# Attention weights split into bf16 pairs on the vector engine, and quantized weights stored in tiles

## The reference

```python
h = einsum('bse,end->bsnd', layernorm(x), proj_weight)      # 16 heads x 64
q = einsum('bsnd,ndh->bsnh', h, attn_weight)
scores = einsum('bsnh,brnh->bsnr', q, h) / 64
w = softmax(scores, axis=-1)
v = einsum('brnd,ndh->brnh', h, value_weight)
x = x + einsum('bsnr,brnh->bsnh', w, v).reshape(b, s, -1) @ out_w.T + out_b

def bitlinear(x, w):       # act_quant: round to 8 bits per row; weight_quant: -1, 0, 1 by mean |w|
    return einsum('bsi,oi->bso', act_quant(x), weight_quant(w))
y = layernorm(x)
x = x + bitlinear(silu(bitlinear(y, w_gate)) * bitlinear(y, w_up), w_down)
```

## Time and profile before

| | us |
|---|---|
| two timed runs | 8569.36 and 8852.18, median 8710.77 |
| the profiled execution | 8584.53 |
| its span on the slowest core (core 3) | 8583.0 |
| spans of all cores | 8447.2 to 8583.0 |
| PE busy | 5073.9 (59%) |
| DVE busy | 2923.0 (34%) |
| ACT busy | 1595.1 (19%) |
| POOL busy | 87.8 (1%) |

### The profile page before, as it was taken

One profiled execution on the slowest core, in us unless ns is written; L12 is line 12 of the kernel. 1 busy time (PEld: TensorE's weight loads), 2 busy tenths in 40 slices (PEclk: granted clock), 3 DMA queues, 4 the chain that ended last, 5 costly groups with the idle time before them and its releaser, 6 DMA issues.

```text
span 8583.0 us, 74830 instructions; the slowest of 8 cores (8447.2 to 8583.0 us)
## 1 busy us (share of the span) xinstructions
PE 5073.9 (59%) x21542; PEld 1955.8 (23%) x21542; DVE 2923.0 (34%) x6992; ACT 1595.1 (19%) x2602; POOL 87.8 (1%) x134
## 2 busy tenths in 40 slices
PE   0015568788887884447878788886354363353443
PEld 0002222222222221222222222222232232232232
DVE  5664431211112114552121212113434524434434
ACT  0000013333332331003333233331000000000000
POOL 0000000000000000000000000000000000000000
PEclk9996677878878886668889889887666566566666
DMA  7640000000000001000000000002343343343343
GB/s 265 235 153 30 30 9 2 5 1 2 4 2 2 1 2 38 30 25 4 2 4 2 5 2 2 1 2 48 71 93 71 62 102 67 66 96 68 82 86 71
DMA packets 837224, 395.55 MB, mean 46 GB/s; under 512 B 803939, under 2 KB 804067, under 8 KB 830692
## 3 DMA queue, kind: packets, MB, share of 16 engines
q1 hardware_dynamic: 827044, 353.00, 17.3%
q0 software_dynamic: 9792, 37.78, 1.2%
HBM read 352.95 MB, written 33.55 MB: 45 GB/s over the span
## 4 chain that ended last, share of the span: by engine, by line
PE 54%; DVE 24%; DMA 8%; issue 7%; DVEq 6%; ACT 0%; SPq 0%; ACTq 0%; POOLq 0%; POOL 0%
PE pb_av L766 23%; PE pb_s L785 10%; PE pb_av L466 5%; PE pf_u L1293 2%; PE pf_g L1287 2%; PE pb_av L662 2%; PE pf_d L1475 2%; PE pf_d L1293 2%; DMA f_wd<-wdq 2%; PE pf_d L1287 2%; DVE ln_lo L484 2%; DVE ln_hi L482 2%; DVE f_guq L1448 1%; DVE f_gr L1439 1%; DVE rr_t L844 1%
## 5 line engine op out<-in xcount | busy, mean ns | idle before, releaser
L826 ACT ACTIVATE w<-pb_s,cbias 128x512 f32<-128x512 f32 x2048 | 1298.0, 685 | 1673.7 <-PE pb_s L785 1673.2
L766 PE MATMUL pb_av<-w,vA 128*65 128x512 f32 x2048 | 1161.5, 650 | 0.0
L766 PE MATMUL pb_av<-w,vB 128*65 128x512 f32 x2048 | 1101.2, 621 | 0.0
L844 DVE RECIPROCAL rr_t<-pb_av 1x512 f32<-1x512 f32 x64 | 210.1, 3320 | 2306.3 <-PE pb_av L766 2306.3
L1475 PE MATMUL pf_d<-f_guq,f_wd 128*128 128x256 bf16 x2048 | 279.4, 307 | 648.2 <-DVE f_guq L1448 542.9
L785 PE MATMUL pb_s<-q_hi,h_hi 64*128 64x512 bf16 x2048 | 448.5, 409 | 260.0 <-DVEq L713 150.5
L1263 ACT ACTIVATE f_si<-f_gr 128x256 f32<-128x256 f32 x256 | 106.9, 417 | 2094.9 <-DVEq L1319 1202.5
L785 PE MATMUL pb_s<-q_lo,h_hi 64*128 64x512 bf16 x2048 | 443.3, 404 | 0.0
L766 PEld LDWEIGHTS pb_av<-w,vB 128*65 128x65 f32 x2048 | 294.9, 144 | 645.7 <-issue 645.7
L785 PE MATMUL pb_s<-q_hi,h_lo 64*128 64x512 bf16 x2048 | 441.6, 402 | 0.0
L644 DVE TENSOR_TENSOR x_tm<-x_tm,pb_av 128x512 f32<-128x512 f32 x256 | 176.1, 688 | 702.1 <-PE pb_av L662 595.7
(11 more groups left out here) (216 smaller groups left out, 5488.3 us busy)
## 6 DMA issues: line engine op xcount, KB each, us to landing
f_wg<-wgq SPq DMA_DIRECT2D x256, 256.0 KB, 3.3
f_wu<-wuq SPq DMA_DIRECT2D x256, 256.0 KB, 3.9
f_wd<-wdq SPq DMA_DIRECT2D x64, 1024.0 KB, 8.1
wraw<-wgT SPq DMA_DIRECT2D x16, 2048.0 KB, 10.4
wraw<-wuT SPq DMA_DIRECT2D x16, 2048.0 KB, 10.0
wraw<-wdT SPq DMA_DIRECT2D x64, 512.0 KB, 4.0
xa<-x_full SPq DMA_DIRECT2D x64, 512.0 KB, 3.2
x_tm<-x_full SPq DMA_DIRECT2D x16, 512.0 KB, 13.8
```

The lines of the kernel that those rows point to most:

```text
L766: last = te.matmul(pb_av[2 + hidx][0:65, 0:512], vb[:, o:o + 65], w32[:, wofs:wofs + 512], start=(rc == 0), stop=(rc == NRC - 1))
L826: a_e.inc(sc.activation(w32[:, slot:slot + 512], pb_s[hidx][:, 0:512], AFT.Exp, bias=cbias[:, 2 * scpar + hidx:2 * scpar + hidx + 1], scal ...
L844: v.reciprocal(rr_t[64:65, hidx * 512:(hidx + 1) * 512], pb_av[2 + hidx][64:65, 0:512])
```

## The change

The change has three parts.

1. The exponentials are split. For every tile of `w32` DVE makes `w_hi` (bf16) and `w_lo` (the rest, bf16), and AV becomes three bf16 matmuls per head instead of one fp32 matmul. The values become pairs too: `vA_hi`, `vA_lo`, `vB_hi`, `vB_lo`, with 1.0 and 0.0 in the last column. AV now waits for the split (`v_w`), and an exponential waits for the split that read its slot, not for AV.
2. The put-off output projection is issued at block 1 of the next loop instead of block 8. In DVE's stream the residual adds stand ahead of the new block of splits.
3. The quantized weights are stored in DRAM as `[128, blocks, row tiles, 128]`, so that the load of a block is one contiguous piece per partition, 2 KB for `f_wg` and `f_wu` and 8 KB for `f_wd`. The write of a tile by POOL now has pieces of 128 columns, 256 bytes each.

```diff
-    wgq_h = nc.dram_tensor("wgq", [E, INNER], BF16, kind="Internal").ap()
-    wuq_h = nc.dram_tensor("wuq", [E, INNER], BF16, kind="Internal").ap()
-    wdq_h = nc.dram_tensor("wdq", [INNER, E], BF16, kind="Internal").ap()
+    wgq_h = nc.dram_tensor("wgq", [128, 32, 8, 128], BF16, kind="Internal").ap()
+    wuq_h = nc.dram_tensor("wuq", [128, 32, 8, 128], BF16, kind="Internal").ap()
+    wdq_h = nc.dram_tensor("wdq", [128, 8, 32, 128], BF16, kind="Internal").ap()
...
                     o_wq.inc(g.dma_start(
-                        out=dst[t * 128:(t + 1) * 128, :],
-                        in_=wqt[:, (t % 2) * 4096:(t % 2) * 4096 + wdt]), t)
+                        out=dst[:, :, t, :],
+                        in_=wqt[:, (t % 2) * 4096:(t % 2) * 4096 + wdt]
+                        .rearrange("p (o c) -> p o c", c=128)), t)
...
-                    for (hp, vb) in ((0, vA), (64, vB)):
+                    for (hp, vh, vl) in ((0, vA_hi, vA_lo), (64, vB_hi, vB_lo)):
                         pav = pb_av[(0 if hp == 0 else 2) + rc % 2]
-                        v.tensor_copy(vb[:, o:o + 64], pav[:, 0:64])
-                        v.memset(vb[:, o + 64:o + 65], 1.0)
+                        v.tensor_copy(vh[:, o:o + 64], pav[:, 0:64])
+                        v.memset(vh[:, o + 64:o + 65], 1.0)
+                        v.drain()
+                        v.tensor_tensor(vl[:, o:o + 64], pav[:, 0:64],
+                                        vh[:, o:o + 64], ALU.subtract)
+                        v.memset(vl[:, o + 64:o + 65], 0.0)
                     v_ve.inc(v.drain())
...
                         for hidx in range(2):
-                            a_e.w(te, bae + 2 * rc + hidx + 1)
+                            v_w.w(te, bvw + 2 * rc + hidx + 1)
...
-                            last = te.matmul(
-                                pb_av[2 + hidx][0:65, 0:512],
-                                vb[:, o:o + 65],
-                                w32[:, wofs:wofs + 512],
-                                start=(rc == 0), stop=(rc == NRC - 1))
+                            for k, (vv, ww) in enumerate(
+                                    ((vh, w_hi), (vh, w_lo), (vl, w_hi))):
+                                last = te.matmul(
+                                    pb_av[2 + hidx][0:65, 0:512],
+                                    vv[:, o:o + 65],
+                                    ww[:, wofs:wofs + 512],
+                                    start=(rc == 0 and k == 0),
+                                    stop=(rc == NRC - 1 and k == 2))
...
-                        if rc == 8 and pend is not None:
+                        if rc == 1 and pend is not None:
                             emit_outproj(te, pend)
...
                             if rc >= 2:
-                                t_av.w(sc, btav + rc - 1)
-                            elif btav > 0:
-                                t_av.w(sc, btav + rc - 1)
+                                v_w.w(sc, bvw + 2 * rc - 2)
+                            elif bvw > 0:
+                                v_w.w(sc, bvw + 2 * rc - 2)
...
+                @blk.vector
+                def _(v):
+                    for rc in range(NRC):
+                        for hidx in range(2):
+                            a_e.w(v, bae + 2 * rc + hidx + 1)
+                            slot = (2 * (rc % 2) + hidx) * 512
+                            v.tensor_copy(w_hi[:, slot:slot + 512],
+                                          w32[:, slot:slot + 512])
+                            v.drain()
+                            v.tensor_tensor(w_lo[:, slot:slot + 512],
+                                            w32[:, slot:slot + 512],
+                                            w_hi[:, slot:slot + 512], ALU.subtract)
+                            v_w.inc(v.drain())
...
                         out=f_wg[:, buf:buf + 1024].rearrange("p (a c) -> p a c", c=128),
-                        in_=wgq_h[:, oc * 128:(oc + 1) * 128].rearrange(
-                            "(a p) c -> p a c", p=128)), oc)
+                        in_=wgq_h[:, oc, :, :]), oc)
...
                             "p (a c) -> p a c", c=128),
-                        in_=wdq_h[:, ec * 128:(ec + 1) * 128].rearrange(
-                            "(a p) c -> p a c", p=128)), ec)
+                        in_=wdq_h[:, ec, :, :]), ec)
```

More of the change, by code:

```diff
@@ L310, in build_program @@
         h_lo = asb("h_lo", [128, 4 * 4096], BF16)
-        vA = asb("vA", [128, NRC * 65], F32)
-        vB = asb("vB", [128, NRC * 65], F32)
+        vA_hi = asb("vA_hi", [128, NRC * 65], BF16)
+        vA_lo = asb("vA_lo", [128, NRC * 65], BF16)
+        vB_hi = asb("vB_hi", [128, NRC * 65], BF16)
+        vB_lo = asb("vB_lo", [128, NRC * 65], BF16)
         stat = asb("stat", [128, 16], F32)
@@ L560, in emit_attention @@
             (aw_f, vw_f, ow_f, aw_hi, aw_lo, vw_hi, vw_lo, ow_hi, ow_lo,
-             q_hi, q_lo, w32, mq_t, cbias, csc, crow,
+             q_hi, q_lo, w32, w_hi, w_lo, mq_t, cbias, csc, crow,
              attn_tm, attn_hi, attn_lo, rr_t, rhib, fbA_t, fbB_t, attnB_s) = T
@@ L751, in emit_attention @@
                 hm = curhead
-                bts, bae, btav = t_s.n, a_e.n, t_av.n
+                bts, bae, btav, bvw = t_s.n, a_e.n, t_av.n, v_w.n
                 bvnm, btat, bvaf = v_nm.n, t_at.n, v_af.n
@@ L763, in emit_av @@
                             wofs = (2 * (rc % 2) + hidx) * 512
-                            vb = [vA, vB][hidx]
+                            vh, vl = [(vA_hi, vA_lo), (vB_hi, vB_lo)][hidx]
                             o = rc * 65
-                            last = te.matmul(
-                                pb_av[2 + hidx][0:65, 0:512],
-                                vb[:, o:o + 65],
-                                w32[:, wofs:wofs + 512],
-                                start=(rc == 0), stop=(rc == NRC - 1))
+                            for k, (vv, ww) in enumerate(
[6 more added lines that the diff above has]
+                                    stop=(rc == NRC - 1 and k == 2))
                         t_av.inc(last)
@@ L935, in build_program @@
                      bsb("w32", [128, 4 * 512], F32),
+                     bsb("w_hi", [128, 4 * 512], BF16),
+                     bsb("w_lo", [128, 4 * 512], BF16),
                      bsb("mq_t", [128, 1], F32), bsb("cbias", [128, 4], F32),
@@ L1238, in _ @@
                         out=f_wg[:, buf:buf + 1024].rearrange("p (a c) -> p a c", c=128),
-                        in_=wgq_h[:, oc * 128:(oc + 1) * 128].rearrange(
-                            "(a p) c -> p a c", p=128)), oc)
+                        in_=wgq_h[:, oc, :, :]), oc)
                     d_fw.inc(sy.dma_start(
                         out=f_wu[:, buf:buf + 1024].rearrange("p (a c) -> p a c", c=128),
-                        in_=wuq_h[:, oc * 128:(oc + 1) * 128].rearrange(
-                            "(a p) c -> p a c", p=128)), oc)
+                        in_=wuq_h[:, oc, :, :]), oc)
             @blk.scalar
```

## The result

The change makes the kernel slower: 1.0345 times the time before, 95% interval 1.0298 to 1.0393 (medians 8577.0 us before, 8823.1 us after). The ratio leaves out executions in which some cores ran slower at a lower TensorE clock, so it isn't the quotient of the medians, which is 1.029. The profiled execution took 8871.6 us, on its slowest core (core 0) a span of 8870.1 us, against 8583.0 on core 3 before. I read the start times of each stage's first and last instruction in the trace, for these two cores and for core 5 of both. The slowest cores alone would mislead: in the first attention stage of before, cores 2 and 3 had a mean granted clock of 0.82 and the other six 0.88, and over the whole span of after, cores 0 to 3 had 0.75 and cores 4 to 7 had 0.77.

A forecast was written before the change was run, and what follows sets the result against it. The prediction took attention, and in it TensorE, to bound the kernel before. From 8585 us, loops +105, value build +160, reading -125 and writing +155 gave 8880 us, range 8700 to 9070.

The forecast's parts named there:

- Writing, +155: Weight quantization: writing tiled weights in 256 B pieces from GpSimd adds 155 us, between ends of +30 and +280.
- the middle between "all fixed" and "4.2 ns a row": GpSimd's issue of weight writes: fixed cost gives +30 us, cost per row up to +280; +155 taken.
- Rival A: Weight writes: 4096 pieces cost GpSimd as much as 128, so writing is +30, total 8755 us; chance 0.24.
- "many us" nor "still at 0.5 us": Signs in POOL's write records: many us at L287 would show the forecast right, still 0.5 us wrong.
- Records stretched by DVE: Weight writes: DVE's two-port instructions stop GpSimd's issue, as 1039 against 539 ns; 60 us more if always.
- Loops, +105: Attention loops: splits on DVE, the moved projection and slow stretches add 105 us to 3047, +65 to +145 by gap length.
- The base of the loops: Attention loops before the change: 95.2 us a loop, 3047 us in all 32, from the profiled execution.
- "DVE becomes the bound": Attention loops at full clock: splits take DVE 2.72 us a block against 2.62 before, 0.10 us slower.
- The second ring: Attention loops: split, AV, scores and exponential in line over two blocks, 2.67 us a block, just under DVE's 2.72.
- Value build, +160: Value build: more small DVE instructions make a block 1.2 us instead of 0.57, +160 us over 256 blocks.
- Reading, -125: Feed-forward weight loads in larger pieces: down projection -110 us, f_wg and f_wu -15, together -125.
- Rivals C and D: Attention loops: C, splits without gaps on DVE, -490 us, chance 0.05; D, TensorE loses full clock, about 10300 us, chance 0.04.

The follow-up runs named there:

- act_write: Kernel after with the quantized weights' writes issued from ACT's queue instead of GpSimd's; weight quantization ends at mean 597.4 us, in after 569.6.
- lag2: Kernel after with AV issued one block later and three slots a head for w_hi and w_lo; median block 2.76 us, as in after.
- spread: Kernel after with one group and one residual add of the put-off projection in each of blocks 1 to 8; ratio to before 1.0277.
- inc_sub: Kernel after without the second drain of each tile's split, the subtract itself signalling; ratio to before 1.0038.
- share: Kernel after with head A's w_hi made by ACT as a second exponential instead of DVE's cast; ratio to before 1.0337.
- vgroup: Kernel after with eight key blocks of values in one PSUM bank and DVE's four instructions once for eight blocks; 8651.6 us.

## Why the prediction was right, and where it wasn't

The direction came out: slower, by 295 us forecast and 287 between the two profiled executions (8880 and 8871.6 us). That the size did too is luck: the writing was priced 146 us too high, and the loops, the reads and two stages together as much too low.

- **Writing, +155: wrong.** It was +9 us at the stage's end (562.9 to 571.8; +7 in the mean over the cores). The step that failed is the middle between "all fixed" and "4.2 ns a row". The rows of before hinted at the first (528 ns for 64 rows, 539 for 128), and 4096 pieces take 1.64 us: (1644 - 539)/3968 = 0.28 ns a piece. Rival A had the mechanism, and of the signs neither "many us" nor "still at 0.5 us" came. Also a piece of 256 B was taken for a transfer of 256 B, and `act_write` shows that this holds for ACT's queue only. The Trainium skill, "DMA: Bandwidth & Descriptors", section "Anatomy of one DMA", says that many descriptors can be emitted before the cost shows. The trace agrees in part: 32 times as many pieces cost three times the record, 1.1 us more. The Trainium skill, "DMA: Bandwidth & Descriptors", section "SWDGE vs HWDGE vs iDMA", gives up to 4096 B as the preferred packet for DMAs issued by GpSimd. The trace agrees: the packets have 4096 B.
- **Records stretched by DVE: right, but harmless.** The median for `wgq` is 3.24 us where 1.64 is the shortest. Before it was 1.28 and 0.53. DVE's waits for the writes stayed (42.0 and 41.2 us).
- **Loops, +105: mechanism right, too small.** It is +177 against core 3. The gap behind the subtract is 187 ns (336.0 us over the 1793 casts that didn't wait for ACT), not the 166 of the earlier trace rows, and cast to subtract 76 ns: 2048 x 23 ns = 47 us. The mean block, 2.80 us, is above its median of 2.76, which makes up for the rest. The start of a loop was right to a tenth (12.1 us, forecast 2.8 + 8.6 + 0.8).
- **The base of the loops.** I took 3047 us as the kernel's own pace. It was that of cores 2 and 3 alone (3051); the other six had 2943 to 2946 us in the same execution. After has 3216 to 3231 us on all eight, though cores 0 to 3 had a granted clock of 0.82 in the first attention stage and cores 4 to 7 had 0.86: with DVE as the bound the loops hardly feel TensorE's clock. So against six of eight cores the loops lose 275 us; the earlier trace rows, where the granted clock was 0.81, described two cores of one execution. The +20 for slow stretches rests on them too.
- **"DVE becomes the bound": right.** `lag2` leaves the block as it is (the loops change by 31 us of 3228), `spread` pays for each add, `inc_sub` gains at once. The second ring, which I put at 2.67 us, fits as well: its terms, with the durations in `inc_sub`, give 2.46 us, and the median block there is 2.47. It only showed once DVE was faster.
- **Value build, +160: right.** It is +162 from 150 to 312 us, and +152 by the stage table (19.1 us for each of the six builds in its row); a block takes 1.19 us for 1.2.
- **Reading, -125:** feed-forward gained 94 to 107 us. f_wd lands in 5.4 us (forecast 5), and the remaining wait is 46.7 us where I had 34. For the clock I had counted 40 us; the busy time of the down projection's matmuls fell by 22 (279.4 to 257.7).
- **Not in the sum:** on core 0 both projection stages are together 42 us longer beyond the value builds. On core 5 they aren't. The granted clock was 0.66 and 0.60 in the two stages on core 0, and 0.70 and 0.65 on core 5; no run tells more of it.

155 - 9 = 146 too much for writing; 72, 31 and 42 too little for loops, reading and the two stages, and 8 too much for the values (152 by the stages): so 295 became 287. Rivals C and D fell: DVE's gaps were there, and granted clock stayed at 0.80 and 0.84 in the two attention stages (0.82 and 0.87 in the earlier trace rows; the first window reaches some 70 us into the next stage, and up to its end, 1251 to 3370, the clock was 0.82):
```profile
1190.00:3440.00 2250.00, 1539.07 (x7488) 480.66 (x7504) 1638.40 (x3692) 674.52 (x1052) 17.89 (x33) 0.80 0.02 4
4090.00:6210.00 2120.00, 1463.64 (x7182) 455.06 (x7197) 1534.96 (x3292) 654.72 (x1020) 16.29 (x30) 0.84 0.01 2
```
But C's lever was real: one of the two drains a tile is not needed, and taking it away gives back 316 us.

## What to carry to other kernels

Work moved off the bounding engine must be priced with its gaps, not its busy time: 2 x 1.12 us of split fits into a block of 2.62, 2 x 1.38 doesn't. Where no later vector instruction reads what one wrote, as with `w_lo` here, try to let it signal itself instead of a drain behind it. Before a base is taken from the slowest core, compare the same stage on the others; and before the bound is moved again, look for the ring behind it, since both `inc_sub` and `share` met one at 2.5 to 2.7 us.

## What the runs showed of the hardware

- A drain that carries the signal costs DVE 0.27 us between a subtract and a cast of 512 columns, against a signal on the subtract itself (0.88 and 0.61 us from start to start, after and `inc_sub`). Without it the next instruction starts 0.08 us before the last one's record ends.
- GpSimd's queue joined 256 B pieces to packets of 4096 B (after), ACT's left them at 256 B (`act_write`). GpSimd's issue took 1.64 us for 4096 pieces and 0.84 for 1024, 0.28 to 0.34 ns for each piece beyond 128.
- 1 MB loads landed in 5.4 us with 8 KB pieces and 8.1 with 256 B.
- DVE's small instructions cost more than their columns: from PSUM 64 columns take 0.22 to 0.23 us, 512 take 0.68 to 0.69 (after, `vgroup`).
